# Router weights broadcast from the on-chip tile, and key products in two strips of the array

## What is computed

```
# L0_ffn: eight experts of width 176 with two chosen per token, and a shared expert of width 704
probs = softmax(x @ router_weight.T); top_v, top_i = top_k(probs, 2); top_v = top_v / top_v.sum()
combine = (one_hot(top_i, E) * top_v[..., None]).sum(axis=1)
for e in range(E):
    gate, up = split(x @ gate_up_proj[e].T)
    out = out + (silu(gate) * up @ down_proj[e].T) * combine[:, e:e + 1]
out = out + sigmoid(x @ shared_gate_w.T) * shared

# L1_ffn: a gated MLP of width 1024 and a product-key memory of 512 experts
queries = (hidden_states @ W_q).reshape(2, n, 64)
routing = einsum('tnd,tdk->tnk', queries, keys)          # keys: 2 x 64 x 64
scores2, idx2 = top_k(routing, 8)                        # then the best 8 of the 64 sums, softmax,
experts_states = einsum('nk,nkh->nh', silu(x . de) * softmax(scores), ue)
mlp = silu(x @ gate_w) * (x @ up_w) @ down_w
```

## Time and profile before

| | us |
|---|---|
| median of 3 runs | 1073.08 |
| lowest and highest | 1072.37 to 1073.54 |
| the profiled execution | 1073.45 |
| its span, first to last instruction | 1071.67 |
| PE busy | 1007.0 |
| DVE busy | 743.6 |
| ACT busy | 622.7 |
| POOL busy | 402.7 |

### The profile page before, as it was taken

The page is one execution under the profiler, slowest core; times in us unless marked ns, Lnnn a source line. Parts: engine busy times, 40 slices in busy tenths (PEclk is TensorE's granted clock), DMA queues, the critical chain, the costliest instruction groups (busy, mean ns, idle before and its releaser), DMA issues. The chain is left out here.

```text
span 1071.7 us, 21337 instructions
## 1 busy us (share of the span) xinstructions
PE 1007.0 (94%) x7186; PEld 833.7 (78%) x7186; DVE 743.6 (69%) x2168; ACT 622.7 (58%) x1559; POOL 402.7 (38%) x380
## 2 busy tenths in 40 slices
PE   8999999999998988899998999999999988889988
PEld 7677887877776557788887788888898875777867
DVE  6677777777755687555557677776777763748984
ACT  2188777777773863333443677777777764224332
POOL 5766667676643011000002635343434421111240
PEclk9999999999999999999998999999999999989999
DMA  5361122201006000654430101110110100001101
GB/s 174 70 189 36 36 60 51 55 17 41 2 2 225 2 2 20 122 139 110 103 83 6 31 16 31 34 29 25 28 36 15 30 6 1 1 1 45 45 30 55
DMA packets 25916, 53.65 MB, mean 50 GB/s; under 512 B 3986, under 2 KB 11218, under 8 KB 24558
## 3 DMA queue, kind: packets, MB, share of 16 engines
q1 hardware_dynamic: 25838, 52.65, 18.7%
HBM read 42.56 MB, written 1.69 MB: 41 GB/s over the span
## 5 line engine op out<-in xcount | busy, mean ns | idle before, releaser
L522 ACT ACTIVATE sb_a_P<-sb_a_nS,sb_a_nm 128x257 f32<-128x257 f32 x256 | 127.6, 507 | 86.5 <-DVE sb_a_nm L633 86.3
L432 POOL TENSOR_TENSOR sb_a_P<-sb_a_P,sb_a_rec 128x512 f32<-128x512 f32 x128 | 129.2, 1040 | 87.6 <-DVE sb_a_rec L644 87.4
L633 DVE CUSTOM_DVE_ANT_0 sb_a_nS<-a_pS,sb_a_mask,sb_a_nsink 128x256 f32<-128x256 f32 x256 | 109.3, 479 | 39.7 <-PE a_pS L781 39.7
L1940 ACT ACTIVATE sb_a_t<-a_pp,sb_a_w 64x512 f32<-64x512 f32 x128 | 87.4, 683 | 17.0 <-PE a_pp L143 9.4
L2013 DVE SCALAR_TENSOR_TENSOR sb_a_t<-a_pp,sb_a_w,sb_a_cs 128x512 f32<-128x512 f32 x64 | 47.8, 746 | 56.0 <-ACT sb_a_t L1940 56.0
L143 PE MATMUL a_pp<-sb_x_high,sb_a_w_low 128*128 128x512 f32 x188 | 80.6, 429 | 5.7 <-DVE sb_a_P L588 3.5
L1879 POOL TENSOR_TENSOR sb_a_qT<-sb_a_t 128x512 f32<-128x512 f32 x32 | 41.3, 1292 | 116.1 <-DVE sb_a_t L2016 116.1
L143 PE MATMUL a_pp<-sb_x_low,sb_a_w_high 128*128 128x512 f32 x188 | 75.0, 399 | 0.0
L143 PE MATMUL a_pp<-sb_x_high,sb_a_w_high 128*128 128x512 f32 x188 | 74.9, 398 | 0.0
L531 ACT COPY sb_xn<-a_pT 128x512 f32<-128x512 f32 x128 | 68.0, 583 | 1.9 <-PE a_pT L795 1.9
L795 PE MATMUL a_pT<-sb_ident,sb_a_P 128*128 128x128 f32 x512 | 68.2, 276 | 0.3 <-ACT sb_xn L531 0.3
(11 more groups left out here) (416 smaller groups left out, 3178.7 us busy)
## 6 DMA issues: line engine op xcount, KB each, us to landing
sb_m_cw<-m_table SPq DMA_DIRECT2D x15, 512.0 KB
sb_a_kr<-sb_a_kall SPq DMA_DIRECT2D x28, 256.0 KB, 3.9
sb_f_w<-f_w SPq DMA_DIRECT2D x12, 384.0 KB, 3.1
sb_m_gu<-m_gu SPq DMA_DIRECT2D x17, 256.0 KB, 6.3
sb_a_w<-a_w SPq DMA_DIRECT2D x16, 257.0 KB, 2.7
sb_m_dn<-m_dn SPq DMA_DIRECT2D x17, 128.0 KB, 7.0
sb_a_w<-a_w SPq DMA_DIRECT2D x8, 259.0 KB, 2.7
sb_a_wo<-a_wo SPq DMA_DIRECT2D x8, 256.0 KB, 2.6
```

What stands on the lines that cost most here:

```text
L432: nc.gpsimd.tensor_tensor(part, part, rec[b % 2][:, h, :].rearrange("p (q o) -> p q o", o=1) .to_broadcast([P, 2, S]), ALU.mult).then_inc( ...
L522: out = nc.scalar.activation(Pm[b % 2][:, h, qt, 0:S + 1], nS[:, h, qt, 0:S + 1], ACT.Exp, bias=nm[b % 2][:, h, qt:qt + 1], scale=-1.0, ac ...
L633: out = nc.vector.tensor_tensor_reduce(nS[:, h, qt, 0:S], pS[h][:, qt * S:(qt + 1) * S], wmask[:, qt, :], -1.0, nsink[par][:, h:h + 1], AL ...
L1940: out = nc.scalar.activation(t2[n][a, :, :].rearrange("p b s -> p (b s)"), pp[n][b, :], ACT.Identity, bias=bias[b])
```

## The change

In experts_0 `few` and its semaphore are gone. The three broadcasts read their row from `combT` itself, one SBUF partition as the source of 128, 48 and 80 rows; the store of `table` follows as before. SP no longer waits between `combT_ready` and the broadcasts.

In memory_1 `QI` has 128 partitions: the queries of the first half of the tokens (which are the first of the two sets) on partitions 0 to 63, those of the second half on 64 to 127, and `keys` lies on 128 partitions in the same way. The key products of the two sets, of 64 rows each, take turns, one on the upper and one on the lower 64 rows of the array. PE waits for all four copies of the queries before the first of them. The up products of tile 0's first half now come behind the key products and not ahead of them. POOL waits for the last of the eight instructions that make xn before its first low part.

```diff
@@ experts_0 @@
-        few = nc.dram_tensor("m0_few", (M0_COLS, T), F32, kind="Internal").ap()
...
-            sp.dma_start(few, combT[:, :]).then_inc(few_out, 16)
-            sp.wait_ge(few_out, 16)
             of_first = M0_I - P
-            sp.dma_start(cw[0][:, :], few[0:1].to_broadcast([P, T])).then_inc(cw_in[0], 16)
-            sp.dma_start(cw[1][0:of_first, :], few[0:1].to_broadcast([of_first, T])).then_inc(cw_in[1], 16)
-            sp.dma_start(cw[1][of_first:P, :], few[1:2].to_broadcast([P - of_first, T])).then_inc(second_cw, 16)
+            row_of = lambda e, rows: combT[e:e + 1, :].rearrange("o (r t) -> o r t", r=1).to_broadcast([1, rows, T])
+            sp.dma_start(cw[0][:, :], row_of(0, P)).then_inc(cw_in[0], 16)
+            sp.dma_start(cw[1][0:of_first, :], row_of(0, of_first)).then_inc(cw_in[1], 16)
+            sp.dma_start(cw[1][of_first:P, :], row_of(1, P - of_first)).then_inc(second_cw, 16)
             sp.dma_start(table, spread_rows).then_inc(table_out, 16)
@@ memory_1 @@
-    "f1": [("f1_wq", [P, KD, P], F32), ("f1_keys", [64, 2, 64], F32), ("f1_iota", [P, 512], F32)]
+    "f1": [("f1_wq", [P, KD, P], F32), ("f1_keys", [P, 64], F32), ("f1_iota", [P, 512], F32)]
...
-        QI = sb("QI", [F1_R, T, 2])
+        QI = sb("QI", [2 * F1_R, NC, 2])
...
             k.wait(pool, "f1")
+            pool.wait_ge(k.norm_of_f1.xn_ready, NT)
...
-                    nc.scalar.copy(QI[:, half * NC:(half + 1) * NC, s], acc[2 + half][s * F1_R:(s + 1) * F1_R, :])\
+                    nc.scalar.copy(QI[half * F1_R:(half + 1) * F1_R, :, s], acc[2 + half][s * F1_R:(s + 1) * F1_R, :])\
...
-            gate_up(0, (0,))
-            for a in range(2):
-                pe.wait_ge(QI_ready, 2 * a + 2)
-                for j in range(NT):
-                    rows_n = QI[:, a * NC + j * (P // 2):a * NC + (j + 1) * (P // 2), :].rearrange("r t s -> r (t s)")
-                    out = nc.tensor.matmul(acc[a][:, j * F1_KEYS:(j + 1) * F1_KEYS], rows_n, keys[:, a, :],
+            gate_up(0, (0,), (0,))
+            pe.wait_ge(QI_ready, 4)
+            for j in range(NT):
+                for a in range(2):
+                    strip = slice(a * F1_R, (a + 1) * F1_R)
+                    rows_n = QI[strip, j * (P // 2):(j + 1) * (P // 2), :].rearrange("r t s -> r (t s)")
+                    out = nc.tensor.matmul(acc[a][:, j * F1_KEYS:(j + 1) * F1_KEYS], rows_n, keys[strip, :],
                                            start=True, stop=True)
             out.then_inc(routed, 1)
+            gate_up(0, (0,), (1,))
             gate_up(0, (1,))
```

More of the change, by code:

```diff
@@ L1406, in experts_0 @@
         cw_in = [sem(f"cw_in{i}") for i in range(2)]
-        few_out, second_cw = sem("few_out"), sem("second_cw")
+        second_cw = sem("second_cw")
         logits, lg_ready, routed, gates, comb_ready = (sem("logits"), sem("lg_ready"), sem("routed"),
@@ L2763, in _, with gate_up @@
                 out.then_inc(queried, 1)
-            def gate_up(n, halves=range(2)):
+            def gate_up(n, halves=range(2), parts=range(2)):
                 pe.wait_ge(w_split, n + 1)
@@ L2769, in gate_up @@
                         pe.wait_ge(h_ready, 2 * n + h - 1)
-                    for bank, off in ((pg[h], 0), (pu[h], D)):
+                    for part in parts:
+                        bank, off = (pg, pu)[part][h], part * D
                         if off and n >= F1_GT:
@@ L2783, in gate_up @@
                                                       PW[:, 4 * h + t, e * P:(e + 1) * P], k.tile["ident"][:, :])
-                    out.then_inc(gated, 1)
+                    if 1 in parts:
+                        out.then_inc(gated, 1)
             def down(n):
@@ L2935, in layouts @@
     out["f1_wq"] = rowm(a["L1_ffn_W_q"])
-    out["f1_keys"] = a["L1_ffn_keys"].transpose(1, 0, 2)
+    out["f1_keys"] = a["L1_ffn_keys"].reshape(P, -1)
     out["f1_iota"] = np.broadcast_to(np.arange(F1_E, dtype=f), (P, F1_E))
```

## The result

The changed kernel took 1106.62 us in the median of four executions (1099.97 to 1108.85), beside 1073.31 for the kernel before (four executions). The ratio is 1.0278, with a 95% interval of 1.0242 to 1.0315; on 1073.3 us that is 26.0 to 33.8 us more. The forecast was 1101.0, or 1.026 times the time before. The profiled execution is the shortest of the four, 1099.97 us with a span of 1098.2, and what follows reads that one: 26.5 us more span than before.

The account below looks back on a forecast made before the run. PE, busy 94% of the span, was taken as the bound, so only its waits and what feeds them count. experts_0 +31.6 and memory_1 -3.7 us give +27.9 on the median 1073.08: 1101.0 us, range 1093 to 1118.

Parts of the forecast that it names:

- The rate of one partition: experts_0 broadcasts: four neighbouring partitions act as one source, which the 16 DMA engines share at 28 GB/s.
- (a): experts_0: a lone partition is no bottleneck, served as DRAM was, so only SP's wait goes; 1068.1 us, chance 0.12.
- (b): experts_0: engines, not partitions, limit, or low partitions together give 84 GB/s; 1071.4 to 1074.5 us, chance 0.05.
- (c): experts_0: sixteen engines on one partition disturb each other; at 20 GB/s 61.4 us for 43.9, 1118.5 us, chance 0.03.
- lower end of 15.4 GB/s: experts_0: one partition's lowest rate, if an engine takes its two partitions one after the other; 1130 us.
- The path in experts_0: Broadcasts, then table, through partitions 0 to 3 in 43.9 us; tile 2's weights queue behind, PE's down product +30.1 us.
- added for the clock: experts_0: 1.5 us added because long idle times let PE's clock fall to half speed.
- The fixed part of 1.3 us: experts_0: time on top of the transfer at the source's rate, taken from the old small copy's 1.88 us.
- The 2.5 us of slack: experts_0, tile 2: PE needed DVE's low half only 2.5 us after it was ready, so +32.6 becomes +30.1 us.
- the lesser of two paths: memory_1: gain at DVE's product is the lesser of PE's 2.6 us (1.7 more if clock holds) and DVE's 4.0.
- the sign that the prediction named for being right: memory_1: the copy of the routing starts some 4 us sooner after xn's first scaling.
- rival (d): memory_1: the key products' strips do not overlap, +1.7 us, 1103.7 us; counted inside the forecast, 0.80 together.

Follow-up runs that it names:

- part 2 of the experiments: Three kernels, against the changed kernel: router rows copied so that each broadcast reads four or sixteen source partitions; 1104.34, 1073.28 and 1070.68 us, one execution each.
- the broadcast alone: Kernel before with only the three broadcasts changed to read combT in SBUF, memory_1 as before: 1109.73 us, ratio 1.0309.
- four neighbours: Changed kernel, but the two router rows stand on four neighbouring partitions each and each broadcast reads all four: 1104.34 us.
- four partitions four apart: Changed kernel, but each broadcast reads its router row from four partitions that lie four apart (16, 20, 24, 28 for expert 0): 1073.28 us.
- sixteen neighbours: Changed kernel, but the router rows are copied to 16 neighbouring partitions each and each broadcast reads all 16: 1070.68 us.

## Why the prediction was right

**The rate of one partition** was the term that decided, and it held. DVE's second product came 470.62 - 451.89 = 18.73 us after the first, which is 524,288 bytes at 28.0 GB/s, the number taken. Rivals (a) and (b) fell by 20 us and more, and (c), 20 GB/s, with them. (For its lower end of 15.4 GB/s the prediction puts 1130 us; 1,228,800 bytes at that rate are 79.8 us, which gives 1137. No chance and no end of the range hangs on it.) Reading by groups of four neighbours, and not by partitions or by engines, was the choice that mattered; part 2 of the experiments shows it was the right reason too.

**The path in experts_0**, its steps as put there:

| step | forecast | measured |
|---|---|---|
| cw0 used by DVE | 450.9 | 451.89 |
| cw1 | 469.6 | 470.62 |
| SP past the table | 476.1 (+32.6) | 477.49 (+34.0) |
| from there to DVE's product of tile 2 | 8.4 | 7.90 |
| PE's down product of tile 2 | 486.6 (+30.1) | 487.68 (+31.1) |
| added for the clock | 1.5 | 0.1 |
| loss at memory_1's start | 31.6 | 31.25 (31.8 from ACT's copy of the turned weights on) |

Two terms were mis-sized and happened to cancel, which was luck. The fixed part of 1.3 us, read off a small copy of 52 KB, 16 KB of it from these partitions, was 451.89 - 430.30 - 18.73 = 2.9 us here, where SP also issued 0.56 us earlier than in the trace of before. And the 1.5 us for the clock were hardly due: it did fall, to 0.50 for 16 us, but inside PE's own waits (three rows of PE above), so it cost nothing behind the last of them. The 2.5 us of slack were right: PE's distance to DVE's product of tile 2 shrank from 4.69 to 2.29 us.

**memory_1**: forecast -3.7, measured -4.8 in this trace. The wait gave 0.9, as put. The key products gave 1.75 (3.71 to 1.96), as put. The step that failed is the lesser of two paths, between 2.6 and 4.0. It took PE's path, 2.6 and perhaps 1.7 more if the clock held behind the key products. The clock held (1.00 from 988 to 992 us, where the earlier trace rows had 0.50), PE's path was out of the way, and DVE's was the bound: 20.4 to 16.1 us, 4.25 less. This includes 0.2 us from the query products (5.39 to 5.16), which leaves the 4.0 that the prediction gives for DVE's path. DVE's copy of the routing came 4.3 us sooner after xn's first scaling (988.18 - 976.59 = 11.6 us, 15.9 before), the sign that the prediction named for being right; rival (d), no overlap of the strips, fell. The stretch up to the end kept 0.5 us more of it, which I can't place.

**The time** came out 5.6 us above the forecast, though the profiled execution is 1.4 us under its own (1101.35). The other three executions took 5.2 to 8.9 us more than it, at a granted clock of 0.966 to 0.970 in place of 0.975. The other traces with a slow broadcast show two places for it: 416 to 428 us, 3.6 us in the broadcast alone, and 490 to 500 us, where the mean clock was 0.83 in the broadcast alone and 0.68 with four neighbours (3.4 and 6.4 of the 10 us at half clock, 1.7 and 3.2 us of work late), and 1.00 in the trace of after. Together that is 5.3 to 6.8 us and would fit; the executions themselves have no trace, so it stays open. The forecast had no term for it, and the range, 1093 to 1118, covered it.

## What to carry to other kernels

Before a row is broadcast by DMA straight from SBUF, count the groups of four neighbouring partitions that hold it, not the engines or the bytes: one group gives about 28 GB/s, so for 1 MB it was cheaper to store 52 KB to DRAM, 1.9 us with the landing, and read back at 269 GB/s: DVE had the first weights 6.6 us after SP's first issue, and 21.6 us after it straight from SBUF. If the wait of such a broadcast is to go, let the engine that turned the data make it: eight more transposes and two copies, with one tile's up products moved ahead of the wait, took the first weights off the path for 1 us of PE's time. A few microseconds in a stretch are best read as the distance between two events of the trace, since the clock moves the whole program by as much between executions.

## What was not expected of the hardware

SP can stand in the issue of a DMA itself. The third broadcast took 15.33 us to issue and the table 8.03, where the same two took 0.42 and 1.04 before. With four neighbours they took 4.18 and 4.14 us, with four partitions four apart 1.26 and 1.25, and with sixteen neighbours 4.23 and 2.15. The source's rate is not all of it, since four neighbours (25 GB/s) and sixteen (100 GB/s) held SP equally long at the third broadcast; what sets the time stays open. It cost nothing here, because SP had nothing to do but wait for the table; a load for another stage queued behind them would have been late by that much.

PE's clock falls in stretches that the edits do not touch differ between executions of equal work: the stretch of 416 to 428 us is at 0.50 to 0.53 in five of the 14 traces, at 0.72 in one and at 0.86 in eight, and the query products take 3.0 or up to 5.5 us. Such falls moved this program by more than most of the edits in memory_1.
